# Keys by head on GpSimd instead of VectorE, and masks in 32-row tiles, in a five-attention kernel with a hand-written order

## The reference

```python
x = L0(x, ctx)     # self attention, +res, norm; cross attention with every 4th key, +res, norm; ffn (gelu), +res, norm
x = L1(x, ctx, m)  # cross attention with key mask m, keys = values; W_out, W_upd on [x, attended], +x, norm
x = L2(x, ctx)     # cross attention, causal mask; + q, norm; ffn, + norm
x = L3(x, ctx, i)  # weights relu(s)^2 where |key - i| <= 1, over max(sum, 1e-6); W_o, + x

# the fourth attention, of L2:
scores = jnp.einsum('bhqd,bhkd->bhqk', Q_, K_) / D_HEAD ** 0.5
scores = jnp.where(jnp.tril(ones(Sq, Sk)), scores, -1e9)
att = jnp.einsum('bhqk,bhkd->bhqd', softmax(scores, -1), V_)
att_h = _layer_norm(att + q, ln_g, ln_b)
```

## Time and profile before

| | |
|---|---|
| median of 3 runs | 193.84 us (194.53, 188.85, 193.84) |
| the profiled execution's own time | 188.99 us |
| its span, first to last instruction | 187.1 us |
| granted TensorE clock | 1.00 of full speed (2.4 GHz) |
| busy: TensorE, VectorE, ScalarE, GpSimd | 175.3, 134.9, 117.7, 38.1 us |

### The profile page before, as it was taken

The page is one execution under the profiler, slowest core; times in us unless marked ns, Lnnn a source line. Parts: engine busy times, 40 slices in busy tenths (PEclk is TensorE's granted clock), DMA queues, the critical chain, the costliest instruction groups (busy, mean ns, idle before and its releaser), DMA issues.

```text
span 187.1 us, 10262 instructions
## 1 busy us (share of the span) xinstructions
PE 175.3 (94%) x4535; PEld 132.1 (71%) x4535; DVE 134.9 (72%) x278; ACT 117.7 (63%) x293; POOL 38.1 (20%) x55
## 2 busy tenths in 40 slices
PE   7889979999899999999999987999979999999995
PEld 3458658777778889778866765677547776777783
DVE  4799947887656898396168988268889459867881
ACT  3357425677777975776883645659386847565663
POOL 8920070414201106301101034103230101100000
PEclk9999999999999999999999999999999999999999
DMA  5997000000000000000000000000000000000012
GB/s 127 307 403 251 4 4 4 5 5 7 4 4 4 4 0 0 5 4 0 5 7 4 4 5 4 4 4 4 4 5 4 4 4 7 0 4 5 25 38 60
DMA packets 4347, 6.24 MB, mean 33 GB/s; under 512 B 592, under 2 KB 3664, under 8 KB 4048
## 3 DMA queue, kind: packets, MB, share of 16 engines
...
q10 hardware_dynamic: 432, 0.17, 0.3%
...
## 4 chain that ended last, share of the span: by engine, by line
PE 82%; DVE 6%; issue 5%; ACT 3%; DMA 2%; ACTq 0%; POOL 0%; POOLq 0%; DVEq 0%
PE bank L359 39%; PE score L362 22%; PE bank L362 12%; PE bank L584 6%; DVE m_col_sb L945 3%; DMA small_sb<-in_small 2%; PE bank L492 1%; DVE k_heads_sb L872 1%; ACT L803 1%; PE bank L645 1%; ACT probs_sb L724 1%; PE bank L689 1%; DVE att_sb L1020 0%; PE bank L440 0%; ACT hid_sb L803 0%
## 5 line engine op out<-in xcount | busy, mean ns | idle before, releaser
L1117 POOL TENSOR_TENSOR rstd_sb<-var_sb,half_sb 128x2 f32<-128x2 f32 x20 | 15.1, 755 | 106.2 <-ACT att_sb L786 79.2
L724 ACT ACTIVATE probs_sb<-score 128x1024 f32<-128x1024 f32 (+1 forms) x28 | 25.9, 961 | 15.8 <-PE score L362 15.6
L945 DVE TENSOR_REDUCE m_col_sb<-score 128x32 f32<-128x2048 f32 (+1 forms) x16 | 30.2, 1890 | 5.8 <-PE score L362 5.2
L359 PEld LDWEIGHTS bank<-v_ext_sb,probs_sb 128*32 128x32 f32 x2112 | 22.2, 110 | 9.5 <-issue 7.9
L359 PE MATMUL bank<-v_ext_sb,probs_sb 128*32 128x18 f32 (+1 forms) x2112 | 26.1, 189 | 1.3 <-issue 1.3
L362 PE MATMUL score<-q_heads_sb,k_kept_sb 32*64 32x256 f32 x512 | 20.1, 386 | 1.0 <-issue 1.0
L359 PE MATMUL bank<-xa_sb,W_sb 128*128 128x256 f32 x62 | 18.4, 409 | 0.4 <-ACT k_kept_sb L749 0.2
L1025 DVE TENSOR_TENSOR att_sb<-bank,rstd_sb 128x256 f32<-128x256 f32 x16 | 6.8, 423 | 14.4 <-POOL rstd_sb L1117 14.3
L786 ACT ACTIVATE att_sb<-bank,eps_sb 128x128 f32<-128x128 f32 x32 | 11.5, 366 | 9.0 <-PE bank L362 8.9
L886 DVE TENSOR_TENSOR q_heads_sb<-q_kept_sb,small_sb 128x1024 f32<-128x1024 f32 x12 | 14.8, 1237 | 0.7 <-ACT q_kept_sb L738 0.7
L584 PE MATMUL bank<-W_sb,att_sb 128*128 128x128 f32 x71 | 14.1, 286 | 1.3 <-DVE att_sb L1020 1.2
...
## 6 DMA issues: line engine op xcount, KB each, us to landing
...
```

What stands on the lines that cost most here:

```text
L359: return pe.matmul(o, l, r, start=start, stop=stop)
L724: act.activation(dst, src, ACT.Exp, scale=SCALE).then_inc(sem("exp"), 1)
L945: dve.tensor_reduce(o, src, AX.X, ALU.max).then_inc(sem("max"), 1)
L1117: pool.tensor_tensor(rstd[:, g, :], var[:, g, :], half[:, 0:NJ], ALU.pow).then_inc(sem("rstd"), 1)
```

## The change

1. `k_heads` of `l1` and `l2` becomes a step of its own, `k_spread`, on GpSimd, with the same operands: eight `tensor_tensor` of 128x1024, with `s` waiting for the semaphore of the new step (`keys_step`). The `k_heads` of `sa` and `ca` stay on VectorE.
2. The masks of `l2` are made with patterns of 32 rows. Each of the old matmuls becomes two, of 256 columns each, one for each half of the 64 keys (in `s`) or queries (in `t`). Row 31 (in `s`) or row 0 (in `t`) of the 32 rows stands for all of the other half. The pattern array grows from 192 to 320 columns.
3. `warm` is a view of `probs`.
4. The list `SCHEDULE` is another one from its seventh line on; one line of it, that of `s/l2/2`, stands below.

```diff
-PATTERNS = ["same", "later", "earlier"]
+PATTERNS = {"query_0": (0, 64), "query_1": (64, 64), "key_0": (128, 64), "key_1": (192, 64), "later": (256, 32), "earlier": (288, 32)}
+PATTERNS_N = 320
...
+def keys_step(name):
+
+    return "k_spread" if name in ("l1", "l2") else "k_heads"
...
-        warm = sb("warm", [128, 512], BF)
+        warm = probs[:, 0, 0:256].bitcast(BF)
...
-        pat = sb("pat", [128, len(PATTERNS), 64])
-        patb = sb("patb", [128, len(PATTERNS), 64], BF)
+        pat = sb("pat", [128, PATTERNS_N])
+        patb = sb("patb", [128, PATTERNS_N], BF)
...
-                pe.wait_ge(sem("k_heads"), nth("k_heads", name, g))
+                pe.wait_ge(sem(keys_step(name)), nth(keys_step(name), name, g))
...
-                                part = rows_of(r // 2, 64)
-                                mm_onto(o.rearrange("p j h k -> p (j h) k"), pattern("same")[part, :],
-                                        pattern("later")[part, :].unsqueeze(1).to_broadcast([64, NJ * HH, T]), start=True)
+                                for c in range(2):
+                                    mm_onto(o.rearrange("p j h k -> p (j h) k")[:, :, 32 * c:32 * c + 32],
+                                            pattern(f"query_{c}")[rows_of(r), :], pattern("later")[rows_of(r), :]
+                                            .unsqueeze(1).to_broadcast([32, NJ * HH, 32]), start=c == 0)
...
-                    for x, r in tiles:
-                        part = rows_of(r // 2, 64)
-                        mm_onto(place(x, r).rearrange("p j h q -> p (j h) q"), pattern("same")[part, :],
-                                pattern("earlier")[part, :].unsqueeze(1).to_broadcast([64, NJ * HH, T]), start=True)
+                    for c in range(2):
+                        for x, r in tiles:
+                            mm_onto(place(x, r).rearrange("p j h q -> p (j h) q")[:, :, 32 * c:32 * c + 32],
+                                    pattern(f"key_{c}")[rows_of(r), :], pattern("earlier")[rows_of(r), :]
+                                    .unsqueeze(1).to_broadcast([32, NJ * HH, 32]), start=c == 0)
...
-                if name == "l2":
-                    dve.wait_ge(sem("s"), nth("s", "sa", g))
...
+                elif step == "k_spread":
+                    if name == "l2":
+                        pool.wait_ge(sem("s"), nth("s", "sa", g))
+                    pool.wait_ge(sem("small_loaded"), 16)
+                    pool.wait_ge(sem("k_kept"), nth("k_kept", name, g))
+                    pool.tensor_tensor(k_heads[HEADS[name]][:, g, :, :],
+                                       k_kept[KEYS[name]][:, g, :].unsqueeze(1).to_broadcast([128, HH, GT]),
+                                       const("head").unsqueeze(2).to_broadcast([128, HH, GT]), ALU.mult
+                                       ).then_inc(sem("k_spread"), 1)
...
-v_even/l2 exp/l2/0/1 v/l3/2 z/l1/3 v/l2/1 exp/l2 v_even/l3/2 var/l1/3 q_heads/l2/2 rstd/l1/3 s/l2/2 v_even/l2/1
...
+v_even/l3/2 v_odd/l2/1 x4_rows/l2 v/l2 v_even/l2 flip/l1/3 k_spread/l2/2 s/l2/2 v_odd/l2 max_parts/l2/1 attT/l1/3
```

More of the change, by code:

```diff
@@ L139 @@
-k_kept/l3/2 k_heads/l2/2 ctx_rows//3 q_heads/l1/3 q/l2 q_kept/l2 max_parts/l1/3 ctx_normed//3 t/l1/2 q_heads/l2
-exp/l1/2 k_heads/l2/3 exp/l1/2/1 z/l1/1 var/l1/1 av/l1/2 av/l1/2/1 s/l2 divide/l1/2 rstd/l1/1 scale/l1/1 flip_x/l1/1
-x4_rows/l2/1 ln/l1/1 m/l1/3 m_row/l1/3 ctx_rows ctx_normed max/l2 flip/l1/2 attT/l1/2 q/l2/1 q_kept/l2/1
-q_heads/l2/1 v/l3 v_even/l3 v_odd/l3 x4_rows/l2 t/l1/3 exp/l1/3 exp/l1/3/1 z/l1/2 var/l1/2 rstd/l1/2 k/l3 k_kept/l3
-av/l1/3 s/l2/1 max_parts/l2 m/l2 scale/l1/2 k/l3/1 k_kept/l3/1 flip_x/l1/2 av/l1/3/1 max/l2/1 v/l3/1 ln/l1/2
@@ L149 @@
-v_even/l3/3 av/l2/1 av/l2/1/1 divide/l2/1 stats/l2/1 v_odd/l3/3 x4_rows/l2/3 v/l2/2 v_even/l2/2 h/g/0/1 rstd/l2/1
-v_odd/l2/2 gelu/g/0/1 m/l2/3 m_row/l2/3 t/l2/2 scale/l2/1 exp/l2/2 y/g x6/g k/l3/3 exp/l2/2/1 flip_x/l2/1 x_sq/l3
-q/l3 k_kept/l3/3 av/l2/2 ln/l2/1 t/l2/3 exp/l2/3/1 q_heads/l3 av/l2/2/1 exp/l2/3 h/g/1 gelu/g/1 divide/l2/2
-stats/l2/2 ms/l3 t/l3 gate/l3/0/1 av/l2/3 rstd/l2/2 scale/l2/2 h/g/1/1 flip_x/l2/2 av/l2/3/1 gate/l3 floor/l3
-divide/l2/3 gelu/g/1/1 y/g/1 x6/g/1 stats/l2/3 ln/l2/2 h/g/2 square/l3/0/1 q/l3/1 q_heads/l3/1 rstd/l2/3 square/l3
@@ new lines @@
+gelu/f/2/1 s/l1/1 q_heads/l1 gelu/f/3 m/l1 m_row/l1 z/f/2 var/f/2 h/f/3/1 gelu/f/3/1 rstd/f/2 max/l1/1
+max_parts/l1/1 t/l1 exp/l1 scale/f/2 m/l1/1 m_row/l1/1 z/f/3 flip_x/f/2 ln/f/2 av/l1 k/l2/1 q/l1/2 exp/l1/0/1
+k_kept/l2/1 q_heads/l1/1 t/l1/1 var/f/3 rstd/f/3 scale/f/3 q_kept/l1/2 exp/l1/1/1 exp/l1/1 k_spread/l1/3 av/l1/0/1
+k/l2/2 k_kept/l2/2 ctx_rows//1 divide/l1 ctx_normed//1 k_spread/l2/1 flip_x/f/3 flip/l1 attT/l1 ln/f/3 q_heads/l1/2
+s/l1/2 z/l1 var/l1 rstd/l1 q/l1/3 av/l1/1 max/l1/2 max_parts/l1/2 scale/l1 av/l1/1/1 divide/l1/1 q_kept/l1/3 s/l1/3
@@ new lines @@
+max/l1/3 ctx_rows//2 ctx_normed//2 flip_x/l1 ln/l1 k/l2/3 m/l1/2 flip/l1/1 m_row/l1/2 k_kept/l2/3 k_spread/l2/3
+max_parts/l1/3 q/l2 attT/l1/1 k/l3/2 q_kept/l2 q_heads/l2 k_kept/l3/2 q_heads/l1/3 t/l1/2 exp/l1/2 exp/l1/2/1 m/l1/3
+m_row/l1/3 z/l1/1 var/l1/1 rstd/l1/1 av/l1/2 ctx_rows av/l1/2/1 divide/l1/2 ctx_normed scale/l1/1 s/l2 max/l2
+flip/l1/2 max_parts/l2 v/l3 v_even/l3 attT/l1/2 v_odd/l3 flip_x/l1/1 ln/l1/1 z/l1/2 var/l1/2 q/l2/1 q_kept/l2/1
+q_heads/l2/1 t/l1/3 exp/l1/3/1 ctx_rows//3 exp/l1/3 k/l3/1 k/l3 k_kept/l3 rstd/l1/2 k_kept/l3/1 scale/l1/2
@@ new lines @@
+av/l2/1 v/l2/3 v_even/l2/3 ln/l2 h/g exp/l2/1/1 s/l2/3 m_row/l2/2 max/l2/3 v_odd/l2/3 av/l2/1/1 v/l2/2 divide/l2/1
+stats/l2/1 rstd/l2/1 gelu/g v_odd/l2/2 v/l3/3 v_even/l3/3 h/g/0/1 gelu/g/0/1 v_odd/l3/3 t/l2/2 exp/l2/2 exp/l2/2/1
+y/g max_parts/l2/3 m/l2/3 m_row/l2/3 scale/l2/1 flip_x/l2/1 ln/l2/1 v_even/l2/2 av/l2/2 x6/g q/l3 q_heads/l3 x_sq/l3
+t/l2/3 exp/l2/3 av/l2/2/1 h/g/1 x4_rows/l2/2 divide/l2/2 exp/l2/3/1 stats/l2/2 rstd/l2/2 scale/l2/2 k/l3/3
+k_kept/l3/3 t/l3 gate/l3 av/l2/3 gate/l3/0/1 ms/l3 floor/l3 gelu/g/1 av/l2/3/1 x4_rows/l2/3 divide/l2/3 stats/l2/3
@@ new lines @@
+flip_x/l2/2 ln/l2/2 h/g/1/1 gelu/g/1/1 h/g/2 gelu/g/2 y/g/1 x6/g/1 square/l3 h/g/2/1 gelu/g/2/1 av/l3 rstd/l2/3
+q/l3/1 square/l3/0/1 q_heads/l3/1 y/g/2 t/l3/1 scale/l2/3 x6/g/2 flip_x/l2/3 x_sq/l3/2 q/l3/2 x_sq/l3/1 ms/l3/1
+ln/l2/3 h/g/3 gate/l3/1 q_heads/l3/2 av/l3/0/1 gate/l3/1/1 gelu/g/3 ms/l3/2 floor/l3/2 floor/l3/1 h/g/3/1 t/l3/2
+divide/l3 square/l3/1 av/l3/1 gate/l3/2/1 gelu/g/3/1 y/g/3 gate/l3/2 x6/g/3 square/l3/1/1 square/l3/2/1 square/l3/2
+av/l3/1/1 divide/l3/1 flip/l3 q/l3/3 av/l3/2 av/l3/2/1 q_heads/l3/3 divide/l3/2 t/l3/3 flip/l3/1 attT/l3 flip/l3/2
@@ L298, in pattern @@
         def pattern(n):
-            return patb[:, PATTERNS.index(n), :]
+            a0, w = PATTERNS[n]
+            return patb[:, a0:a0 + w]
         def X(x):
```

80 lines of the change are left out of this document (38 added, 42 removed).

## The result

| | before | after |
|---|---|---|
| median in the same session | 191.34 us (187.23 to 194.53, 4 runs) | 195.75 us (194.38 to 199.31, 4 runs) |
| profiled execution | 188.99 us, span 187.1 | 195.49 us, span 193.7 |
| mean granted clock in it | 1.000 | 0.982 |

The ratio is 1.039 (95% interval 1.024 to 1.054): slower, and outside the predicted range (185.3 to 193.8). Ratios leave out executions in which the granted clock was disturbed for longer: here 188.85 and 187.23 us before, mean 188.0, stand against 195.49, 194.38 and 196.02 after, mean 195.3, which is 7.3 us more.

A forecast was written before the change was run, and what follows sets the result against it. TensorE, busy 175.3 of 187.1 us, was taken as the bound. -2.5 (masks) - 1.3 + 0 + 0.6 + 0.1 + 0.5 = -2.6 us gave 186.4 profiled, 191.2 from the median; range 185.3 to 193.8.

The forecast's parts named there:

- Masks, -2.5: Fourth attention's eight mask blocks on TensorE: 32-row tiles cut each from 0.56 to 0.24 us, 2.5 us in all.
- rival 4: Fourth attention's s mask blocks stay at 0.56 us or more, only t gains, 1.25 us; 187.6 or 192.5 us; chance 0.14.
- The 64 extra matmuls are in it: Fourth attention's masks: the 2.5 us gain was held to include already the cost of the 64 added matmuls.
- Issue: TensorE stops that the profile puts down to nothing: 1.3 us in three stops noted, no change entered in the sum.
- Keys: Third and fourth attention: eight key operations leave VectorE (9.8 us) for GpSimd, 2.5 us each, hidden by being queued early.
- rival 3: GpSimd gets in the way: k_spread stretches q_heads, delays s/l2/2 and rstd; 193.1 or 197.9 us; chance 0.09.
- I count it as free: k_spread/l1 of group 0, ahead of rstd/sa on GpSimd: no cost, hardly any slack, up to 2.5 us later there.
- Holding up: Third and fourth attention: q_heads and k_spread meet at some three places, each making GpSimd or VectorE up to 1.2 us late.
- Waits gone, -1.3: TensorE's waits for the m_row copy (0.9 us) and gelu (0.4) vanish in the new order.
- New wait at the score buffer, +0.6: Between t/l1/3 and s/l2/1, 1.35 us of TensorE work against 1.94 us of exponentials: 0.6 us of new wait.
- L1020, 0: TensorE's 1.2 us wait for the fourth attention's normalized rows: cost put at 0, bounds -1.2 and +0.6.
- Tail, +0.5: From t/l3/3 to the end: av/l3/2 moved ahead leaves less TensorE work beneath the gate chain, +0.5 us.

## Why the prediction was wrong, point by point

- **Masks, -2.5.** The block size was right (0.22 to 0.24 us; rival 4 is out), and it was worth what I said in TensorE's own work. The sentence that failed is "The 64 extra matmuls are in it". They are 128 more instructions, in stretches where TensorE already takes 256 in less than 3.35 us, and they push all later code along the grid. By themselves the masks cost 2.4% at their place and 1.8% at a better one, and did not gain 1.3%. How much of this is the denser code and how much the shift was not separated. I had even weighed a fixed cost per matmul and thrown it out, since the earlier trace rows show none. Both are true: 128 run in 1.23 us, 10 ns each, but no more than 128 in 3.45 us, 27 ns each. (By the Trainium skill, "TensorEngine Tiling (Array Packing)", Instruction Overhead, 60 cycles a matmul would be an estimated 25 ns at 2.4 GHz. The runs have something near it as the pace of the supply, 27 ns, and not as the cost of one matmul, 10 ns.)
- **"Issue", 3.4 us before, left out of the sum, which prices its change at 0.** This is the term that made the kernel slower. It became 8.3: the largest single term, and the row stood first in the earlier trace rows. I had read 1.3 of it and passed over the lines of 1.1 and 1.0. The masks are not the only thing that raises it: the new order with the old masks has 6.3 and 6.2 us.
- **Keys.** A `k_spread` is 1.89 us (one 2.87), not 2.5, and `s/l2/2` never waited for it: the cover was there, rival 3's mechanism is out. "I count it as free" was wrong all the same, for a queue I priced only once: in the old order all eight key steps cost 1.1 to 1.4%, and with the third attention's back on VectorE and two others late nothing of it is left. How much of this the new order keeps was not separated.
- **Holding up.** The rule was right, the victim not. I looked at `q_heads` (one, at 96.0 us, took 1.56 in place of 1.22) and left out `max_parts`, a tiny instruction with both inputs in SBUF. That is why VectorE fell by 5.0 us and not by 9.8: the first halves of `max_parts` went from 3.0 to 5.8 us in sum, the normalizations of the fourth attention from 3.3 to 4.3. TensorE waited only some 0.4 us behind `max_parts` here, so this explains little of the loss. In the changed kernel, where a key step runs from 30.59 and from 104.99:

```profile
30.93 1.59 DVE L959 TENSOR_TENSOR m_part_sb<-m_col_sb,minus_sb 128x32 bf16<-128x32 f32 x1
...
105.34 1.58 DVE L959 TENSOR_TENSOR m_part_sb<-m_col_sb,minus_sb 128x32 bf16<-128x32 f32 x1
```

- **Waits gone, -1.3.** Half: `m_row` 0.9 to 0.6, gelu gone, but five new waits of 0.3 to 0.4 each. **New wait at the score buffer, +0.6:** right, 0.6 (L733). **L1020, 0:** 1.2 to 0.9, but not as I reasoned: `x4_rows` still lies over four of these normalizations (it starts at 147.94 and 158.21, and they take 0.74 to 0.90 us each, not 0.34). **Tail, +0.5:** from the last gate (183.39) to the end 10.3 us, against 9.6: near, but partly by luck, since 183.5 to 186.9 of it ran at 1.2 GHz, which the forecast did not have.
- **The clock.** I took the profiled execution's full clock for both kernels. The mean over the runs was 0.99 for the kernel before (21 of one session) and 0.97 for the changed one. In the changed kernel's trace it fell right behind the two stops of 2.02 and 1.40 us, worth 3.5 us at most. That the stops cause the falls was not tested.
- **The range.** Its high end, 193.8, was taken from the median before, 193.84. The comparison that the ratio makes starts from 188.0, and from there the miss is 9.9 us (7.3 more, not 2.6 less). Rival 3 had the right direction for a reason that did not occur. It called 8 us "three times what rows 5 give", but the earlier trace rows is VectorE's 1.24 us; three times holds against my own 2.5.
